# Two layers of attention and mixing on one core: the second attention's queries and keys are placed through DRAM

## What is computed

```python
xq = (x @ wq + bq).reshape(B, S, H, D)
xk = (x @ wk + bk).reshape(B, S, KV, D)
xv = (x @ wv + bv).reshape(B, S, KV, D)
q = _rope(xq, cos, sin)
k = _rope(xk, cos, sin)
k = jnp.repeat(k, REP, axis=2)
v = jnp.repeat(xv, REP, axis=2)
scores = jnp.einsum('bqhd,bkhd->bhqk', q, k) / jnp.sqrt(jnp.float32(D))
probs = jax.nn.softmax(scores.astype(jnp.float32), axis=-1)
out = jnp.einsum('bhqk,bkhd->bqhd', probs, v).reshape(B, S, E)
```

## Time and profile before

| | us |
|---|---|
| median of 3 runs | 1701.98 |
| lowest, highest | 1697.08, 1704.78 |
| profiled execution, own time | 1695.3 |
| its span | 1693.5 |
| PE busy | 1268.1 (75%) |
| DVE busy | 1021.7 (60%) |
| POOL busy | 756.1 (45%) |
| ACT busy | 634.5 (37%) |

### The profile page before, as it was taken

How to read it: one execution, slowest core, us unless ns; L and a number is a source line. 1 busy time by engine, 2 the same in 40 slices (tenths; PEclk the granted TensorE clock), 3 DMA queues, 4 the chain that set the end, 5 groups by cost and what they waited for, 6 DMA issues and landing times. The chain is left out here.

```text
span 1693.5 us, 18606 instructions
## 1 busy us (share of the span) xinstructions
PE 1268.1 (75%) x6071; PEld 894.7 (53%) x6071; DVE 1021.7 (60%) x1700; ACT 634.5 (37%) x1198; POOL 756.1 (45%) x742
## 2 busy tenths in 40 slices
PE   2768999999999999999999986588008998951000
PEld 0557767767767777777677665476003333430000
DVE  4644665556646566566565565643108888537888
ACT  0323333333333343344343323332004777743233
POOL 1337656765756667576666655531000003041017
PEclk8889999999999999999999997787556999975555
DMA  4111122122122211221211122005580000000001
GB/s 168 52 57 38 50 76 81 50 64 75 51 74 71 65 48 58 68 63 50 75 57 50 38 76 87 1 0 65 71 85 22 2 3 2 2 1 0 0 0 50
DMA packets 71649, 82.29 MB, mean 49 GB/s; under 512 B 6729, under 2 KB 40681, under 8 KB 71554
## 3 DMA queue, kind: packets, MB, share of 16 engines
q1 hardware_dynamic: 69682, 78.38, 17.9%
q10 hardware_dynamic: 1872, 2.72, 0.4%
HBM read 70.68 MB, written 2.28 MB: 43 GB/s over the span
## 5 line engine op out<-in xcount | busy, mean ns | idle before, releaser
L1155 DVE TENSOR_REDUCE nm<-banks 128x2 f32<-128x1024 f32 x128 | 152.0, 1220 | 24.5 <-PE banks L726 23.5
L1618 POOL TENSOR_TENSOR sw<-sw,sinT 128x512 f32<-128x512 f32 x80 | 103.2, 1290 | 142.1 <-ACT sw L1348 142.1
L1397 ACT ACTIVATE yTh<-yF 128x512 fp32r<-128x512 f32 x64 | 40.5, 632 | 325.7 <-DVE yF L1014 325.7
L1630 POOL TENSOR_TENSOR dec<-gb,gcol 128x512 f32<-128x512 f32 x64 | 70.4, 1100 | 201.9 <-DVE Sd L980 194.2
L1501 ACT ACTIVATE Pb<-banks 128x512 f32<-128x512 f32 x256 | 134.9, 601 | 47.8 <-PE banks L747 47.4
L726 PE MATMUL banks<-ksT,qsT 48*128 48x512 f32 x256 | 67.4, 478 | 92.9 <-DVE nm L1155 70.9
L1673 POOL TENSOR_TENSOR acc<-acc,hh 128x512 f32<-128x512 f32 x8 | 10.5, 1317 | 255.2 <-DVE hh L1056 255.2
L579 PE MATMUL banks<-st,qt 128*128 128x128 f32 x384 | 82.2, 298 | 52.9 <-DVE Sd L980 27.7
L527 PE MATMUL banks<-hTh,wgh 128*128 128x512 f32 x256 | 121.7, 475 | 0.0
L952 DVE SCALAR_TENSOR_TENSOR gs<-tg,banks 128x512 f32<-128x512 f32 x64 | 44.0, 688 | 119.1 <-ACT tg L1355 119.1
L527 PE MATMUL banks<-hTh,wqh 128*128 128x512 f32 x256 | 108.1, 422 | 0.0
(11 more groups left out here) (303 smaller groups left out, 3444.4 us busy)
## 6 DMA issues: line engine op xcount, KB each, us to landing
gb<-g_scr SPq DMA_DIRECT2D x64, 256.0 KB, 3.5
raw<-in_wmod SPq DMA_DIRECT2D x40, 256.0 KB, 2.7
raw<-in_wo SPq DMA_DIRECT2D x32, 256.0 KB, 2.8
raw<-in_wq SPq DMA_DIRECT2D x31, 256.0 KB, 2.7
raw<-in_wg SPq DMA_DIRECT2D x31, 256.0 KB, 2.7
qsT<-hl SPq DMA_DIRECT2D x96, 64.0 KB
mt<-mods_scr SPq DMA_DIRECT2D x12, 256.0 KB, 16.9
stg<-in_wmod SPq DMA_DIRECT2D x2, 1024.0 KB
```

The lines of the kernel that those rows point to most:

```text
L1155: ve.tensor_reduce(nm[:, b, i, p:32:16], pairs[z_][:, :].rearrange("p (g t) -> p g t", g=2), AX.X, ALU.max, negate=True).then_inc(*v_nm.up ...
L1618: po.tensor_tensor(s_[:, :], s_[:, :], sinT[:, :], ALU.mult).then_inc(*g_rope.up("sin", kind, t, n))
L1630: po.tensor_tensor(dec[:, :, :], gb[s % 2][:, :, :], bc(gcol[:, t % 2, heads(t), n], 2, 128), ALU.subtract).then_inc(*g_dec.up("sub", s))
```

## The change

Queries: a unit's high part (two buffers) and its rest (two buffers) are written to a DRAM tensor `d_q`, in eight DMAs of 64 rows by 2 KB (128 KB). They are read back in six DMAs of 16 rows by 16 KB (256 KB): the high part twice, the rest once. SP waits for the landing of the writes (`d_dh`, `d_dr`) before it issues the reads. Keys: two writes of 128 rows (256 KB) to `d_k`, then six reads of 16 rows by 8 KB (128 KB). The order of the columns of the weights, of the tables and of the biases is altered to match (`wide`, `inner`, `key_cols`), and four query tiles of 4 heads become two of 8. `high` and `low` now wait for the previous user's writes to DRAM, not for its placing. `gates` moves from ahead of `attentions` into it, to quad 4. `bias(0)` and `bias(1)` move from ahead of the merged streams, and from behind `conv(9)`, to behind `conv(2)` and `conv(5)`.

```diff
-    qsTs = [[over(past_p + 16 + 8 * n, f"qsT0{n}", [128, 4, 512], F32R) for n in range(4)],
-            [over((64, 72, 16, 24)[n], f"qsT1{n}", [128, 4, 512], F32R) for n in range(4)]]
+    qsTs = [[over(past_p + 16 + 16 * m, f"qsT0{m}", [128, 8, 512], F32R) for m in range(2)],
+            [over((64, 16)[m], f"qsT1{m}", [128, 8, 512], F32R) for m in range(2)]]
...
+    d_q = nc.dram_tensor("q_scr", (2, 2, 2, 2, 2, 64, 512), F32, kind="Internal").ap()
+    d_k = nc.dram_tensor("k_scr", (2, 2, 128, 512), F32, kind="Internal").ap()
...
-        return ap.rearrange("p (n q h r) -> p h n r q", q=4, h=2, r=8)
+        return ap.rearrange("p (n q h r) -> p h n r q", q=8, h=2, r=8)
...
             if prev:
-                ve.wait_ge(*d_pl[prev]("all"))
+                ve.wait_ge(*d_dr[prev]("lo"))
+                if prev[1] < 2:
+                    ve.wait_ge(*d_dh[prev]("hi"))
...
             if u == 2:
+                sp.wait_ge(*a_part(b, u, 0))
+                sp.dma_start(d_k[b, 0], h_[0][:, :].bitcast(F32)).then_inc(*d_dr[b, u].up("hi"))
+                sp.wait_ge(*v_part(b, u, 0))
+                sp.dma_start(d_k[b, 1], h_[2][:, :].bitcast(F32)).then_inc(*d_dr[b, u].up("lo"))
                 sp.wait_ge(*g_vp("ones", b))
+                sp.wait_ge(*d_dr[b, u]("lo"))
                 for s_ in (0, 2, 1):
...
+                        r0, last = 64 * g + 16 * s_, s_ == 1 and g == 1
+                        src = d_k[b, s_ % 2].rearrange("(y x) t -> y x t", x=8)[:, 4 * g:4 * g + 4, :]
+                        sp.dma_start(ksTs[b][r0:r0 + 16, :, :].bitcast(F32), src).then_inc(*(d.up("all") if last else d.up(s_, g)))
                 return
             for n in range(2):
                 sp.wait_ge(*a_part(b, u, n))
...
+                for m in range(2):
+                    src = h_[n][64 * m:64 * m + 64, :].bitcast(F32)
+                    sp.dma_start(d_q[b, u, 0, m, n], src).then_inc(*(d_dh[b, u].up("hi") if n and m else d_dh[b, u].up(n, m)))
+            for n in range(2):
+                sp.wait_ge(*v_part(b, u, n))
+                for m in range(2):
+                    src = h_[2 + n][64 * m:64 * m + 64, :].bitcast(F32)
+                    sp.dma_start(d_q[b, u, 1, m, n], src).then_inc(*(d_dr[b, u].up("lo") if n and m else d_dr[b, u].up(n, m)))
+            for x in range(2):
+                sp.wait_ge(*(d_dr[b, u]("lo") if x else d_dh[b, u]("hi")))
+                for m in range(2):
+                    src = d_q[b, u, x, m].rearrange("h (r q) t -> (h r) (q t)", q=8)
+                    for s_ in ((0, 1), (2,))[x]:
+                        dst = qsTs[b][m][64 * u + 16 * s_:64 * u + 16 * s_ + 16, :, :].bitcast(F32)
+                        sp.dma_start(dst, src).then_inc(*(d.up("all") if x and m else d.up(m, s_)))
...
+            if part == 2:
+                E.bias(0, None), (yield)
+            if part == 5:
                 E.bias(1, E.bank()), (yield)
...
+            if Q == 4:
+                E.gates()
...
-        E.bias(0, None)
         merged(stream(E, second_front), merged(stream(E, starts, 0), stream(E, weights2))).rest()
...
-        E.gates()
```

More of the change, by code:

```diff
@@ L261, in build @@
     d_col = dma_sig("d_col")
+    d_dh = {(b, u): dma_sig(f"d_dh{b}{u}") for b in range(2) for u in range(2)}
+    d_dr = {(b, u): dma_sig(f"d_dr{b}{u}") for b in range(2) for u in range(3)}
     d_pl = {(b, u): dma_sig(f"d_pl{b}{u}") for b in range(2) for u in range(3)}
@@ L720, in pass_a @@
                     pe.wait_ge(*d_pl[b, u]("all"))
[L721 removed]
+            q_, k_ = qsTs[b][p // 8], ksTs[b]
             for g in range(2):
@@ L1476, in high @@
             if prev:
-                ac.wait_ge(*d_pl[prev]("all"))
+                ac.wait_ge(*d_dr[prev]("lo"))
+                if prev[1] < 2:
+                    ac.wait_ge(*d_dh[prev]("hi"))
             else:
@@ L1710, in tables @@
             for j in range(4):
-                p = po.tensor_copy(rep_[part][:, j, :].rearrange("p (n r q) -> p n r q", r=8, q=4), bc(bc(src[:, j, :], 2, 4), 1, 4))
+                p = po.tensor_copy(rep_[part][:, j, :].rearrange("p (n r q) -> p n r q", r=8, q=8), bc(bc(src[:, j, :], 2, 8), 1, 2))
             p.then_inc(*g_vp.up("rep", part))
@@ L1729, in bias @@
                 for h in range(2):
-                    po.tensor_copy(abp[:, 2 * g + h, :].rearrange("p (n r q) -> p n r q", r=8, q=4), wide(ab1[:, 256 * g:256 * g + 256])[:, h, :, :, :])
+                    po.tensor_copy(abp[:, 2 * g + h, :].rearrange("p (n r q) -> p n r q", r=8, q=8), wide(ab1[:, 256 * g:256 * g + 256])[:, h, :, :, :])
             for n in range(2):
                 for h in range(2):
-                    p = po.tensor_copy(abp[:, 4 + n, 64 * h:64 * h + 64].rearrange("p (g r c) -> p g r c", g=2, r=8),
+                    p = po.tensor_copy(abp[:, 4 + n, 64 * h:64 * h + 64].rearrange("p (r g c) -> p r g c", g=2, r=8),
                                        key_cols(ab1[:, 512:640])[:, h if n == 0 else 1 - h, :, :, :])
```

14 lines of the change are left out of this document (7 added, 7 removed).

## The result

The changed kernel takes 1643.42 us (median of 4 runs, 1641.26 to 1644.52) against 1699.53 us (median of 4, 1688.65 to 1704.78) for the kernel before, run beside it: a ratio of 0.968, 95% interval 0.963 to 0.973. The forecast was 1649 us in a range of 1627 to 1673. The profiled execution took 1641.26 us, its span 1639.5 us, 54.0 us less than the span before.

The account below looks back on a forecast made before the run. The stall ahead of the second attention, where placing DMAs into 8 rows drain, was taken as the bound. First scores moving from 1288.0 to 1233.8 gain 54.2 us, less 1 for gates: 1702 - 53 = 1649 us, range 1627 to 1673.

Parts of the forecast that it names:

- The hole, and what ends it: Between layer 0's loop and the second attention, PE idles while placing DMAs drain; the end moves as the first scores (1288.0) move.
- The unit of 17.3 us: Placing one query unit: writes 3.0 us, empty queue 1.5 us, six reads at 123 GB/s 12.8 us.
- the rows written limit: In placing, the number of rows written sets the DMA rate: 62 GB/s for 8 rows, 123 for 16 in query reads.
- The key unit of 7.3 us: Placing one batch's keys: writes 1.5 us, landing and issue 2.0 us, reads at 206 GB/s 3.8 us.
- Biases 2.8 us: Ahead of placing, moving POOL's bias copies gives DVE and POOL time back: placing starts at 1140.0 instead of 1142.8.
- The sum: From placing's start at 1140.0, key units, query units, broadcasts and maxima add up to first scores at 1233.8 instead of 1288.0.
- Gates 1 us, maxima hidden 28 us deep: Moved gates cost 1 us at quad 4; DVE's maxima, 1188.5 to 1205.7, lie hidden 28 us deep under the DMAs.
- Rival 1: Placing reads of 16 neighbouring rows drain no faster than 8, at 62 GB/s: 1715 us with gates; chance 0.11.
- Rival 2: Placing reads not limited by rows, at 352 GB/s, or query reads helped by alternating blocks: 1629 us; chance 0.17 for both.
- Rival 3: SP's waits for DRAM landings and half-rate writes cost 22 us in placing: 1671 us; beyond 1672, or Rival 4 with it, 0.10.
- Rival 4: Only the moved gates count, placing no shorter: gain 11 us, 1691 us; chance 0.10 together with Rival 3 beyond 1672.
- The Trainium skill's rule: Ports reached by a DMA's rows set placing's rates: 104 GB/s for rows 0 to 15, writes at 196; about 1675 us.

## Why the prediction was right, step by step

**The hole, and what ends it.** Right. Everything that was gained but 5 us lies between the loop's end and the first scores, and the attention kept its length (206.2 us).

**The unit of 17.3 us.** 16.8 and 16.3. The reads were put at 123 GB/s and ran at 127 to 132. The number was right for a wrong reason: "the rows written limit" would give eight rows in steps of four half of what sixteen neighbours have, and they had more. What counts is how many bytes of one DMA go to the same port. Neighbouring rows have four on each, 8 as well as 16 of them, and 16 reach twice as many ports, so the doubling held. It held by luck, because the 16 rows are neighbours as the 8 were: in steps of four they had 187 GB/s in the window above.

**The key unit of 7.3 us.** Wrong in one term: 206 GB/s was 131 after, as the block of 128 KB reads alone has it (131). The 103 GB/s that it was doubled from does not belong to the order of the rows. The keys of batch 0 in the kernel before are placed in that order too, and from their first issue at 1142.8 to their landing at 1156.1 their 0.79 MB took 13.3 us, about 70 GB/s if 2 us of it are landing; 64 KB from SBUF into 8 rows in turn, alone, gave 71. Why batch 1's ran at 103 in the earlier trace rows is open. By these rates the term cost some 2 us a unit, 4 in all.

**Biases 2.8 us.** Wrong here: 0. The conversions fell from 3.95 to 1.81 us, but in the profiled execution PE's lower clock (0.51 against 1.00 before) took the time back, and on the kernel before the queue did. Where the clock was higher, placing did start 2.9 us earlier.

**The sum.** From the start of placing to the first scores 93.8 us were forecast and 96.2 measured: by the rates the keys some 4 us more, the four query units some 3 us less, the rest in small waits. With the missing 2.8, D was forecast at 158.2 and came at 163.4. That 5.2 us was made good by luck, by what the sum could not hold: a loop that ended 3.6 us earlier in that execution, and an attention 1.4 us shorter, at a clock of 0.97 instead of 0.95, where 1 us of loss stood in the sum. So the own time, forecast 1642 and measured 1641.3, is closer than the steps are. The median came 5.6 us lower than forecast mostly since I had added the 6.7 us by which the profile before lay under its median; the changed kernel's profile lies 2.2 us under its own.

**Gates 1 us, maxima hidden 28 us deep.** DVE's first maximum came at 1190.9 (1188.5 forecast), and PE idled 27.1 us for the transfer of the maxima; at quad 4 the tanh took 0.19 us, and DVE waited 0.2 us for it.

**Rivals.** Rival 1, 16 rows no faster than 8: its price was real, as the reads of 8 rows show (D 213.9), its condition was not. Rival 2, rows that do not limit: the alternation it hoped for, alone, made 15.3 us of 16.4 and, for 128 KB reads, 14.4 of 15.9, not 1.6 times the rate. Rival 3: writes ran at 302 to 330 GB/s in windows of 4 us that hold little else, and of a unit's 16.3 to 16.8 us the reads take 12.1 (1.57 MB at 130 GB/s) and the writes 3.2 to 3.5, so that no more than 1.5 is left for the landings. Rival 4: 11 us forecast for the gates alone, 13.4 measured. The Trainium skill's rule (SBUF — State Buffer, Door 1: The DMA port swizzle), by which it would have been 1675: its map of the ports orders all that was measured, but its 104 GB/s was 127 to 132 in this kernel, and its 196 GB/s for 64 rows is exceeded by those writes, which follow each other on rows of either half.

## What to carry to other kernels

When transfers bound a stage, look first at which rows one DMA writes, and spread its bytes over the ports: with two rows of 16 on a port instead of four the same reads took 9.3 to 10.1 us instead of 15.3 to 16.4, by an edit of the step alone. Then ask what stands ahead of what the next stage waits for: here moving 18 large reads behind one small transfer was worth as much as the better rate (14.4 us of D against 13.8). And measure such parts from a mark inside the kernel, as the time ahead of it varied by 12 us.

## What the runs showed of the hardware

- Six reads of 256 KB from DRAM into 16 rows, with the last landing: 9.3 to 10.1 us with at most two rows of a DMA on a port, 13.7 to 14.8 with three, 15.3 to 16.4 with four. Four or eight neighbouring rows take 15.7 to 15.9 us for a quarter or half of the bytes, eight rows with two on a port 9.7 and 9.8, with one 7.7. A DMA share of 1.0 says nothing here: in windows of two of these blocks it was 1.09 at 117 GB/s and 1.10 at 225.
- DMAs in turn on blocks of different ports gain little: 15.3 against 16.4 us for six reads of 256 KB, 14.4 against 15.9 for twelve of 128 KB, 20.5 against 25.9 for twenty of 64 KB from SBUF; inside the kernel 127 to 132 GB/s.
- Eight broadcasts of 256 KB were issued in 3.7 us behind six reads of 16 rows that still drained, in 14.4 us behind twelve reads of 8 rows, and in 16.7 us behind placing DMAs of 8 rows.
- Two DVE conversions of 128x256 took 3.95 us beside POOL's small copies, 1.81 beside none of them and 1.07 later on.
- The same attention took 206.2 us at a granted clock of 0.97 and 212.8 us at 0.92.
